# Four score banks and three maximum banks, in place of three and four, in the attention of a macaron block

## The reference

```python
x = x + 0.5 * ffn(layernorm(x))          # 256 -> 1024, butterfly, gelu, butterfly, -> 256
# attention, 16 heads of size 16, 4096 positions, causal
scores = einsum('bhqd,bhkd->bhqk', Q, K) / sqrt(16)
scores = where(causal, scores, -inf)
attn = einsum('bhqk,bhkv->bhqv', softmax(scores), V)
x = x + einsum('bhsv,hdv->bsd', attn, WO)
x = x + 0.5 * ffn(layernorm(x))
```

## Time and profile before

| | |
|---|---|
| Median of 3 runs | 1914.11 us (1913.44 to 1917.26) |
| Profiled execution | 1913.25 us |
| its span, first to last instruction | 1911.5 us |
| Granted TensorE clock, share of full speed | 0.995 over the span |
| Attention with maxima beside it | about 360 to 1646 us |
| the stretch 500 to 1640 us, busy: PE / VectorE / ScalarE | 1139.85 / 1108.58 / 1035.55 us of 1140 |

### The profile page before, as it was taken

The page is one execution under the profiler, slowest core; times in us unless marked ns, Lnnn a source line. Parts: engine busy times, 40 slices in busy tenths (PEclk is TensorE's granted clock), DMA queues, the critical chain, the costliest instruction groups (busy, mean ns, idle before and its releaser), DMA issues.

```text
span 1911.5 us, 62638 instructions
## 1 busy us (share of the span) xinstructions
PE 1869.8 (98%) x24312; PEld 1310.3 (69%) x24312; DVE 1634.6 (86%) x3631; ACT 1416.7 (74%) x2884; POOL 562.6 (29%) x1056
## 2 busy tenths in 40 slices
PE   4999999899999999999999999999999999999999
PEld 3788888666666666666666666666666666679998
DVE  7756666799999999999999999999999999747662
ACT  5312221589898998989999998999999899875433
POOL 4100100032232333223233322323332232235444
PEclk9999999899999999999999999999999999999999
DMA  7111221212112111211121121111112121101110
GB/s 204 52 54 53 76 82 54 79 42 54 40 51 45 48 46 41 56 40 51 47 47 45 41 55 41 52 47 46 46 41 55 42 52 34 56 26 67 67 45 23
DMA packets 82840, 102.43 MB, mean 54 GB/s; under 512 B 16752, under 2 KB 45168, under 8 KB 82544
## 3 DMA queue, kind: packets, MB, share of 16 engines
q1 hardware_dynamic: 81920, 98.03, 18.3%
q10 hardware_dynamic: 624, 0.40, 0.1%
HBM read 68.46 MB, written 29.36 MB: 51 GB/s over the span
## 4 chain that ended last, share of the span: by engine, by line
PE 94%; DVE 3%; ACT 1%; DMA 1%; POOL 0%; issue 0%; SPq 0%; POOLq 0%; ACTq 0%; DVEq 0%
PE PS L1385 31%; PE PS L1369 30%; PE PS L1254 9%; PE PS L1204 8%; PE PS L1234 7%; PE PS L1433 5%; PE PS L1310 1%; PE PS L1170 1%; PE PS L1228 1%; DVE OA L1008 1%; DMA PG<-w_exp_t 1%; ACT OA L698 0%; POOL QT L667 0%; DVE OA L912 0%; ACT OA L742 0%
## 5 line engine op out<-in xcount | busy, mean ns | idle before, releaser
L788 ACT ACTIVATE PG<-PS 128x512 f32<-128x512 f32 (+3 forms) x2304 | 1135.0, 568 | 113.3 <-PE PS L1369 84.6
L1032 DVE TENSOR_REDUCE MXP<-PS 128x1 f32<-128x512 f32 x1686 | 1041.5, 681 | 23.7 <-PE PS L1254 16.8
L1254 PE MATMUL PS<-KT,QT 48*128 48x512 f32 (+5 forms) x2304 | 782.6, 430 | 2.7 <-DVE MXP L1032 2.2
L1369 PE MATMUL PS<-QT,KT 50*128 50x512 f32 (+3 forms) x2304 | 732.2, 423 | 2.1 <-DMA QT<-MT 1.5
L1385 PE MATMUL PS<-PG,VH 128*17 128x128 f32 x16896 | 652.8, 275 | 0.5 <-POOL PG L623 0.2
L1385 PEld LDWEIGHTS PS<-PG,VH 128*17 128x17 f32 x16896 | 432.8, 97 | 201.9 <-issue 178.2
L1369 PEld LDWEIGHTS PS<-QT,KT 50*128 50x128 f32 x2304 | 359.1, 184 | 271.8 <-ACT PG L788 198.6
L1254 PEld LDWEIGHTS PS<-KT,QT 48*128 48x128 f32 (+1 forms) x2304 | 373.9, 185 | 22.4 <-DVE MXP L1032 8.9
L1028 DVE CUSTOM_DVE_ANT_0 PS<-PS,MASK 128x128 f32<-128x128 f32 (+3 forms) x512 | 242.0, 511 | 38.6 <-PE PS L1254 35.8
L623 POOL TENSOR_SCALAR_AFFINE_SELECT PG<-PG 128x128 f32<-128x128 f32 x512 | 144.2, 292 | 407.4 <-ACT PG L788 396.8
L716 ACT ACTIVATE PG<-PS,GB 128x512 f32<-128x512 f32 x128 | 90.2, 706 | 154.6 <-PE PS L1204 154.6
(11 more groups left out here) (118 smaller groups left out, 1536.6 us busy)
## 6 DMA issues: line engine op xcount, KB each, us to landing
QT<-q_parts SPq DMA_DIRECT2D x256, 64.0 KB
KT<-k_parts SPq DMA_DIRECT2D x256, 64.0 KB
q_parts<-OA SPq DMA_DIRECT2D x16, 512.0 KB, 2.8
k_parts<-OA SPq DMA_DIRECT2D x16, 512.0 KB, 3.7
QT<-q_parts SPq DMA_DIRECT2D x256, 32.0 KB
KT<-k_parts SPq DMA_DIRECT2D x256, 32.0 KB
o_parts<-OS SPq DMA_DIRECT2D x128, 64.0 KB
OA<-o_parts SPq DMA_DIRECT2D x32, 256.0 KB
```

Source lines behind the costliest of these rows:

```text
L788: nc.scalar.activation(PB[u % P_BUFFERS][:, q0:TILE], bank(s_bank(u))[:, q0:TILE], ACT.Exp, scale=1.0 / DH ** 0.5).then_inc(exp_done, 1)
L1032: nc.vector.tensor_reduce(dst, bank(b), AX.X, ALU.max).then_inc(mx_red, 1)
L1254: mm(bank(b, w), q[0:rows, (BT * place(j) + qs) * P:(BT * place(j) + qs + 1) * P].bitcast(f32r), k[0:rows, c * TILE:c * TILE + w].bitcast( ...
L1369: mm(bank(s_bank(u))[:, q0:TILE], kt[0:SM, kb * P:(kb + 1) * P].bitcast(f32r), qt[0:SM, place(j) * TILE + q0:(place(j) + 1) * TILE].bitcas ...
```

## The change

One bank, bank 3, moves from the maxima to the scores. The scores rotate over banks 0 to 3, the maxima over 4, 5 and 7. No instruction is added, removed or reordered; what changes is whose end some matmuls wait for. S of unit u waits for the exponential of unit u-4 in place of u-3. M of unit u waits for the reduction or copy of unit u-3 in place of u-4. The last units still rotate over five banks.

```diff
-S_BANKS = 3
+S_BANKS = 4
-MAX_BANKS = (4, 5, 7, 3)
+MAX_BANKS = (4, 5, 7)
-        LAST_BANKS = [(MX_UNITS + i) % S_BANKS for i in range(S_BANKS)] + [MAX_BANKS[3], MAX_BANKS[2]]
+        LAST_BANKS = [(MX_UNITS + i) % S_BANKS for i in range(S_BANKS)] + [MAX_BANKS[2]]
```

## The result

| | before | after |
|---|---|---|
| Median of 4 runs | 1913.78 us (1912.28 to 1917.26) | 2027.11 us (2025.82 to 2028.28) |
| Span of the profiled execution | 1911.5 us | 2026.0 us |

The account below looks back on a forecast made before the run. VectorE was taken to set the pace, 83.8 us per head. Idle time of 8.4 us per head in place of 1.7, times 15.4 heads, added 103 us to 1914: 2017, shaded to 2014; whole range 1962 to 2042.

Parts of the forecast that it names:

- the likeliest case: Whole kernel: slower through VectorE's idle time, 2014 us, own range 1995 to 2035, 62% chance.
- The chain: End of reduction R2, to M2, over the values to the next M0, to its reduction: 1.81 us.
- The fourth score bank: S2's wait for ScalarE's exponential goes; VectorE can gain at most 1.7 us per head, 26 us.
- The copied groups: Seven groups per head whose third unit is copied: VectorE idle 0.53 us each on average, 3.7 us together.
- The diagonals: Groups with narrow diagonal units: VectorE idle 2.0 us per head in five groups, 0.95 in two more.
- ScalarE's copy: M2 behind a copied unit waits for the copy; delay mostly covered, 0.5 us per head added.
- The full groups: Of the other 34 groups per head, about twenty lose 0.06 us each: 1.2 us.
- the shading: Total lowered from 2017 to 2014 us, since VectorE's 0.62 us steps behind a copied unit give more cover.
- the 1.7 of the waits: VectorE's idle time per head before the change, from its 23.4 us of waits for TensorE in the stretch.
- the smaller loss: Rival: M2 to M0 shrinks to 1.04 us everywhere, chain 1.64 us; 1965 us, 18% chance.
- the larger: Rival: ScalarE's copy isn't covered, each copied unit costs its whole 0.45 us more; 2055 us, 9% chance.
- the overtaking loads: Rival: values' weight loads slip ahead of a waiting M2, taking 0.47 us off the chain; 1908 us, 3% chance.

Follow-up runs that it names:

- the two kernels with tied banks: Kernel before, its four maximum banks fixed to places in the group: two by turns for M0, 2025.61 us; two by turns for M2, 1946.37 us.
- longer values: Four value products of 64 columns added for one full unit per group: on the changed kernel 2052.63 us, on the kernel before 1943.69 us.
- the kernel with three and three: Changed kernel with the fourth score bank taken away again, so three score and three maximum banks, bank 3 idle: 2026.06 us.
- without copies: No copied maxima, VectorE reduces all from PSUM: on the changed kernel 2009.75 us, on the kernel before 1920.67 us.
- two edits: Changed kernel with half of full units' value products left out, 2022.95 us; changed kernel with value products of 32 columns for 128, 2137.69 us.
- the kernel with the spare bank at M2: Kernel before with maximum banks fixed to places: M0 bank 4, M1 bank 5, M2 banks 7 and 3 by turns; 1946.37 us.

## Why the prediction was right

**The time.** 2014 us was forecast and 2027 measured: +100 for +113, inside the likeliest case's own range. That it is this close owes something to luck, as the terms below show: some were too high and others too low.

**The chain.** Its steps measured as predicted: release 0.04 us, M2 to M0 1.22, M0 to reduction 0.56, together 1.82 for 1.81. That it ran through M2 is shown by the two kernels with tied banks: four banks with M2's wait kept, 2026 us; with that wait gone, 1946. That it ran through the values is shown by the places with longer values. The changed kernel by itself shows it as well. Once per head, a group after a tile's end holds five units of values. In the kernel before M2 to M0 is 1.65 us there too, and VectorE doesn't stop; in the changed kernel it stands idle 0.47 us, though both groups are full:

```profile
983.66 0.18 PEld L1254 LDWEIGHTS PS<-KT,QT 48*128 48x128 f32 x1 [0.36 <-DVE MXP L1032]
984.09 1.01 PEld L1385 LDWEIGHTS PS<-PG,VH 128*17 128x17 f32 x28 [0.24 <-issue]
985.31 0.18 PEld L1254 LDWEIGHTS PS<-KT,QT 48*128 48x128 f32 x1
```

```profile
985.87 2.48 DVE L1032 TENSOR_REDUCE MXP<-PS 128x1 f32<-128x512 f32 x4 [0.47 <-PE PS L1254]
```

**What bounds the kernel before.** The prediction had VectorE alone setting the pace. The scores' circle was as long, 82 us per head, as the longer values showed. It did no harm to the forecast: the kernel with three and three keeps that circle and takes as long as the changed kernel, so the chain through M2 is the longer one by then.

**The fourth score bank.** S2's real waits went, as forecast, and that gave nothing, as the kernel with three and three shows.

**The copied groups,** 3.7 us per head forecast. The idle time behind the seven copied units, taken from the trace place by place, is 0.64, 0.63, 0.63, 0.63, 0.54, 0.42 and 0.22 us, also 3.7. The way there was not quite right. I took 0.16 us off where the values hold diagonal units, since those are 18 recorded rows and not 24. They took 0.57 us all the same (912.28 above), and the last two places came out shorter mostly because VectorE had just stood idle ahead of the copied unit.

**The diagonals,** 3.0 us forecast (2.0 and 0.95), 3.7 measured. Behind a narrow group the next M0 is mostly a diagonal one too, and a masked reduction starts 0.72 us behind the weight load, not 0.56. This term came out 0.7 us too low.

**ScalarE's copy,** 0.5 us forecast. M2 behind a copied unit was released 0.05 us behind the end of the copy at four of the seven places, and 0.11 to 0.14 behind it at the other three. The idle time two groups on is 0.36 us at one place of the seven (without copies 0.04 there), and at the others the work at hand covered it: 0.4 in all. (The traces have 106 copies in all, not 107.)

**The full groups,** 1.2 us forecast, nearly nothing of it as idle time. VectorE's busy time per head rose by 0.6 us instead, from 81.5 to 82.1 (the windows' busy time over their 1959 and 1803 maxima). Most of that is lost overlap, and most of it at the places with idle time, since a reduction that follows a gap doesn't overlap the last. That the reductions of copies and the idle time just before cover the full groups is how I read the timeline; no run tests it by itself.

**Not foreseen:** 0.5 us per head in the group with five units of values behind a tile's end, shown above, and 0.2 in one with four, where M2 to M0 is 1.43 us. Another 0.3 behind the narrow unit that ends a group was there before the change too.

A head became 7.3 us longer, from 83.8 to 91.1, by the starts of its first score; times 15.4 that is 112 of the 114.5 us between the two spans. The remaining 2.4 us lie ahead of the first score, in one execution of each. I had 6.7 us per head. The missing 0.6 make 9 us of the 13 that the forecast was low, and the shading from 2017 to 2014 makes 3 more; it went the wrong way. The 0.6 are what is left of misses both ways: 0.7 too low in the diagonals and 0.7 not foreseen, against 0.6 too high in the full groups, 0.1 in the copy, and an idle time before the change of 2.3 us per head when every gap is counted, not the 1.7 of the waits. Of the rivals, the smaller loss falls because a full M2 with three units of values never had less than 1.18 us behind it (1.0 only with two or one unit, in three groups of 48), the larger because the copy's delay was mostly covered, and the overtaking loads because no value load came before M2 was released, and none nearer than 0.25 us behind M2's own.

**What stays open.** That a longer values' stretch costs time with three maximum banks is shown, place by place. That a shorter one would give the time back was not: of two edits one left its length as it was and the other lost the clock. The 33 us of the kernel with the spare bank at M2 were not taken apart.

## What to carry to other kernels

The depth of a rotation isn't a number of banks but a cover: add up what must pass from the moment a bank comes free until the next result built on it, with everything that stands in the queue behind the waiting instruction, and compare it with the work that the consumer has meanwhile. Here 1.81 us stood against 1.70 in a full group and 1.11 in a short one, and it is the short groups that pay. When a bank can be spared, ask which place in the group is followed by the long block in the queue. If the spare is tied to one place, it belongs there: 1946 us against 2026 at another. Letting all four banks rotate did better than either, 1914 us.

## What the runs showed of the hardware

Narrowing the value products from 128 to 32 columns, with all instructions kept, took the granted clock from 1.00 to 0.50 for the whole attention, and made the kernel 11% slower; TensorE had been granted 1.00 from 200 to 330 us, ahead of the attention. Two more things were new to me. Of products packed into four column groups, 12 recorded rows take as long as 24 (0.56 and 0.57 us); each unit more or less in the column groups changes the stretch by 0.22. And reductions that follow each other without a gap can still lose 0.09 us at a place, when the next bank comes just in time.
